# A message ring, one-hots shared with ScalarE and attribute sums moved one pass earlier in a graph network's two gather passes

## The reference

```python
# second layer: sum over the edges that end in a node, and their count
h = features * (deg_out ** (-0.5))[:, None] @ weight
rst = segment_sum(h[src], dst) * (deg_in ** (-0.5))[:, None] + bias
# third layer: a message of each edge
msg = relu(x[src] + edge_attr)
agg = segment_sum(msg, dst)
h = relu((x + agg) @ W1 + b1) @ W2 + b2
# fourth layer, input norm: needs edge_attr summed by node, and edge_attr.T @ edge_attr
h = concatenate([x[col], edge_attr], axis=1)
h = relu(_bn(h @ W1a, g1a, b1a))
```

## Time and profile before

| | us |
|---|---|
| median of three executions | 9768.53 |
| profiled execution, its own time | 9783.38 |
| its span, first to last instruction | 9781.0 |
| second pass, first gather to last `add_block` | 2960.3 to 5054.7 |
| third pass, first gather to last `add_block` | 5109.5 to 7282.1 |

### The profile page before, as it was taken

One profiled execution on the slowest core, in us unless ns is written; L12 is line 12 of the kernel. 1 busy time (PEld: TensorE's weight loads), 2 busy tenths in 40 slices (PEclk: granted clock), 3 DMA queues, 4 the chain that ended last, 5 costly groups with the idle time before them and its releaser, 6 DMA issues. The chain is left out here.

```text
span 9781.0 us, 179091 instructions
## 1 busy us (share of the span) xinstructions
PE 6958.7 (71%) x25668; PEld 5296.4 (54%) x25669; DVE 5640.9 (58%) x22552; ACT 2074.7 (21%) x8123; POOL 6775.9 (69%) x7038
## 2 busy tenths in 40 slices
PE   2676667675768888888845555555567888888886
PEld 1555555554546666666633333333345666666664
DVE  8777777776984444444455555555554444444444
ACT  4344444443120000000002222222221222221222
POOL 0677777776737777777757777777745777777773
PEclk8555555555655555555555555555565555555556
DMA  6333333333642222222212222222212333333334
GB/s 109 96 105 105 106 105 109 103 108 94 138 93 64 55 55 55 55 55 53 57 40 54 55 53 53 53 53 53 54 23 74 80 80 82 80 82 80 82 80 34
DMA packets 625950, 724.44 MB, mean 74 GB/s; under 512 B 403289, under 2 KB 431609, under 8 KB 624766
## 3 DMA queue, kind: packets, MB, share of 16 engines
q1 hardware_dynamic: 394414, 429.07, 16.5%
q0 software_dynamic: 216064, 278.76, 12.9%
q10 hardware_dynamic: 14544, 8.74, 0.5%
HBM read 576.22 MB, written 139.85 MB: 73 GB/s over the span
## 5 line engine op out<-in xcount | busy, mean ns | idle before, releaser
L1293 POOL DMA_INDIRECT arena<-node_table,idx x3328 | 3165.0, 951 | 1091.6 <-issue 788.5
L1231 PE MATMUL banks<-arena,onehot 128*128 x7040 | 2497.3, 472 | 1245.2 <-DVE onehot L1171 608.5
L1231 PEld LDWEIGHTS banks<-arena,onehot 128*128 128x128 f32 x7040 | 1758.4, 311 | 1879.6 <-issue 1673.7
L1414 POOL DMA_INDIRECT arena<-node_table,arena x1760 | 1665.3, 946 | 552.0 <-issue 378.8
L978 POOL DMA_INDIRECT sorted_edges<-arena,idx x1664 | 1616.4, 971 | 615.7 <-issue 575.2
L1171 DVE TENSOR_SCALAR onehot<-iota_row,block_base,edge_tables 128x128 f32<-128x128 f32 x3520 | 1251.8, 357 | 608.5 <-ACTq L1277 464.1
L923 PE MATMUL banks<-arena,onehot 128*128 x3520 | 1103.9, 424 | 563.2 <-DVE onehot L872 550.3
L923 PEld LDWEIGHTS banks<-arena,onehot 128*128 128x128 f32 x3520 | 883.6, 314 | 783.2 <-issue 776.5
L1179 DVE TENSOR_TENSOR arena<-arena,banks 128x65 f32 (+1 forms) x3520 | 895.5, 254 | 583.4 <-PE banks L1231 543.7
L1390 PE MATMUL banks<-arena 128*128 128x64 f32 x3520 | 1214.1, 448 | 0.0
L1385 PE MATMUL banks<-arena 128*64 128x65 f32 x3520 | 843.0, 343 | 396.2 <-ACT arena L1401 387.5
(11 more groups left out here) (291 smaller groups left out, 6021.2 us busy)
## 6 DMA issues: line engine op xcount, KB each, us to landing
arena<-sorted_edges SPq DMA_DIRECT2D x220, 524.0 KB
arena<-in_attr_t SPq DMA_DIRECT2D x208, 512.0 KB
arena<-sorted_edges SPq DMA_DIRECT2D x110, 528.0 KB, 4.3
arena<-row_keys SPq DMA_DIRECT2D x110, 512.0 KB
arena<-in_attr_pairs SPq DMA_DIRECT2D x104, 512.0 KB
arena<-node_table,idx POOLq DMA_INDIRECT x3328, 2.4
arena<-node_table,arena POOLq DMA_INDIRECT x1760, 2.4
sorted_edges<-arena,idx POOLq DMA_INDIRECT x1664
```

Of the source, the lines that this page charges most:

```text
L1231: nc.tensor.matmul(to, m.onehot[:, j % 4, :], rows, start=True, stop=True).then_inc(s["summed"], 1)
L1293: nc.gpsimd.indirect_dma_start(slot(j), None, m.table, bass.IndirectOffsetOnAxis(ap=m.idx[:, j:j + 1], axis=0)).then_inc(gathered[j % 32], 16)
L1414: nc.gpsimd.indirect_dma_start(slots[:, j % SLOTS, 0:D], None, m.table, bass.IndirectOffsetOnAxis(ap=rec_i[:, j % SLOTS, REC_DST:REC], axis=0)
```

## The change

- The sums of the edge attributes by node move from the third pass to the second. The second pass's ring slot is now 129 floats wide (`WIDE`): gathered row, attribute row, a one. SyncE loads the attributes straight into the ring, in pieces of 64 floats. Its products have 129 columns, and a block's sums stand 130 floats apart (`STEP`).
- The Gram matrix moves from the second pass to the third: TensorE multiplies the attribute tile j with itself before step j, for j below 1664, and at every sixteenth waits for the attributes of its chunk.
- In the third pass, messages are made by step and not by tile: VectorE adds gathered row and attributes of the step's own tile into a ring of eight (`messages`), ScalarE applies the relu there, TensorE multiplies 64 columns. So there are 1760 messages where there were 1664.
- VectorE waits for landed tiles at each eighth step in the third pass too. SyncE does the counting, tile by tile, between its own loads. VectorE loads 25 numbers of the plan at each eighth step (eight blocks, eight tiles, eight slots, one last tile) where it loaded 16.
- ScalarE makes the one-hot of each odd step as relu(1 - |lane + offset|): four small activations for the offsets at every eighth step, after loading 16 numbers of the plan, and two activations of 128 x 128 for each odd step.
- GpSimd waits on `landed` at each eighth gather in both passes.

```diff
-            if layer == 1:
-                v.memset(m.pair[:, :, 0:RW], 0.0).then_inc(s["blank"], 1)
-            def add_attr(i, j):
-                c = j // CH
-                dve.wait_ge(gathered[j % 32], i * (RING // 32 * 16) + j // 32 * 16 + 16)
-                if j % CH == 0:
-                    dve.wait_ge(attr_in[c], i * 16 + 16)
-                v.tensor_tensor(slot(j), slot(j), m.third_ring[:, 1, j * D:(j + 1) * D], ALU.add).then_inc(s["sum"], 1)
+            def add_attr(base, j, slots):
+                k = base + j
+                dve.wait_ge(s["summed"], ahead(k - 8, SLACK))
+                v.tensor_tensor(m.messages[:, j % 8, :], rows[:, bass.ds(slots[j] * D, D)], attrs[:, bass.ds(slots[j] * D, D)],
+                                ALU.add).then_inc(s["sum"], 1)
...
+                            last = bounded_values(nc, ENG.DVE, plan[32:33, bass.ds(base + j + 7, 1)], TP - 1)[0]
                             blocks += group(nc, ENG.DVE, plan, 0, base + j, SPARE - 1)
                             tiles += group(nc, ENG.DVE, plan, 1, base + j, TP - 1)
+                            if layer == 2:
+                                slots += group(nc, ENG.DVE, plan, 2, base + j, RING - 1)
+                            dve.wait_ge(s["landed"], last + 1 + EARLY)
+                        if layer == 2:
+                            add_attr(base, j, slots)
+                        if layer == 1 or j % 2 == 0:
+                            match(base, j, tiles, blocks)
...
+        def count(engine, i, j):
+            i, j = i + j // RING, j % RING
+            if j % CH == 0:
+                engine.wait_ge(attr_in[j // CH], i * 16 + 16)
+            engine.wait_ge(gathered[j % 32], i * (RING // 32 * 16) + j // 32 * 16 + 16)
+            engine.sem_inc(s["landed"], 1)
...
+                def rounds(i, last):
+                    for c in range(CHUNKS):
+                        if c + 1 < CHUNKS:
+                            load(sp, i, c + 1)
+                        elif not last:
+                            load(sp, i + 1, 0)
+                        for j in range(c * CH + 8, min(c * CH + CH + 8, RING) if last else c * CH + CH + 8):
+                            count(sp, i, j)
...
+            def add_gram(i, j):
+                if j % CH == 0:
+                    pe.wait_ge(attr_in[j // CH], i * 16 + 16)
+                attr = attrs[:, j * D:(j + 1) * D]
+                nc.tensor.matmul(m.psum[GRAM][0:D, 0:D], attr, attr, start=False, stop=False, skip_group_check=True)
+            with pe.Fori(0, ROUNDS) as i:
+                for j in range(RING):
+                    if layer == 2:
+                        add_gram(i, j)
+                    step(i * RING, j, numbers)
...
+                def aim(base, j):
+                    blocks = group(nc, ENG.Activation, plan, 0, base + j, SPARE - 1)
+                    tiles = group(nc, ENG.Activation, plan, 1, base + j, TP - 1)
+                    act.wait_ge(s["odd"], base + j + EARLY)
+                    for q in range(1, 8, 2):
+                        a_.activation(m.place[:, q:q + 1], targets[:, bass.ds(tiles[q], 1)], ACT.Identity, scale=-1.0,
+                                      bias=m.block_base[:, bass.ds(blocks[q], 1)]).then_inc(s["aimed"], 2)
+                    act.wait_ge(s["aimed"], base + j + 8)
+                def steps(base, units):
+                    for j in range(0, units, 2):
+                        if j % 8 == 0:
+                            aim(base, j)
+                        odd = j + 1
+                        apart = m.junk[:, odd // 2 % 2, :]
+                        a_.activation(apart, m.iota_row[:, :], ACT.Abs, bias=m.place[:, odd % 8:odd % 8 + 1]).then_inc(s["apart"], 2)
+                        relu(base + j, j)
+                        act.wait_ge(s["apart"], base + j + 2)
+                        act.wait_ge(s["summed"], base + odd - 3 + SLACK)
+                        settle(act)
+                        a_.activation(m.onehot[:, odd % 4, :], apart, ACT.Relu, scale=-1.0, bias=m.ones[:, 0:1]).then_inc(s["odd"], 2)
+                        relu(base + odd, odd)
```

More of the change, by code:

```diff
@@ new lines, in _ @@
+            if layer == 1:
+                with sp.Fori(0, ROUNDS) as i:
+                    for c in range(CHUNKS):
+                        load(sp, i, c)
+            else:
+                def rounds(i, last):
+                    for c in range(CHUNKS):
+                        if c + 1 < CHUNKS:
[4 more added lines that the diff above has]
+                            count(sp, i, j)
+                sp.sem_inc(s["landed"], EARLY)
+                load(sp, 0, 0)
+                for j in range(8):
+                    count(sp, 0, j)
+                with sp.Fori(0, ROUNDS - 1) as i:
+                    rounds(i, False)
+                rounds(ROUNDS - 1, True)
@@ L1250, in _ @@
-            with pe.Fori(0, ROUNDS) as i:
-                beats(i)
+                if layer == 1:
+                    if j % 8 == 0:
+                        numbers += group(nc, ENG.PE, plan, 2, k, RING - 1)
+                    frm = m.second_ring[:, bass.ds(numbers[j] * WIDE, WIDE)]
+                else:
+                    pe.wait_ge(s["message"], k + 1)
+                    frm = m.messages[:, j % 8, :]
+                if layer == 1:
+                    pe.wait_ge(s["onehot"], ahead(k, EARLY))
+                else:
+                    pe.wait_ge(s["odd" if j % 2 else "onehot"], ahead(k, EARLY))
@@ L1263, in _ @@
             a_ = nc.scalar
-            act.sem_inc(s["message"], EARLY)
-            if layer == 2:
-                a_.activation(m.pair[:, :, D:2 * D], m.zero[:, 0:D].unsqueeze(1).to_broadcast([P, NB, D]),
+            if layer == 1:
+                a_.activation(m.pair[:, :, D:WIDE], m.zero[:, 0:RW].unsqueeze(1).to_broadcast([P, NB, RW]),
                               ACT.Copy).then_inc(s["blank"], 1)
-                with act.Fori(0, ROUNDS) as i:
-                    for j in range(RING):
-                        act.wait_ge(s["sum"], i * RING + j + 1 + 2 * CH)
-                        a_.activation(slot(j), slot(j), ACT.Relu).then_inc(s["message"], 1)
-            else:
                 act.sem_inc(s["landed"], EARLY)
@@ L1275, in _, with relu @@
                     for j in range(RING):
-                        act.wait_ge(gathered[j % 32], i * (RING // 32 * 16) + j // 32 * 16 + 16)
-                        act.sem_inc(s["landed"], 1)
+                        count(act, i, j)
+            else:
+                def relu(k, j):
+                    act.wait_ge(s["sum"], k + 1)
+                    row = m.messages[:, j % 8, :]
+                    a_.activation(row, row, ACT.Relu).then_inc(s["message"], 1)
+                act.sem_inc(s["odd"], EARLY)
+                def aim(base, j):
[8 more added lines that the diff above has]
+                    for j in range(0, units, 2):
+                        if j % 8 == 0:
+                            aim(base, j)
[8 more added lines that the diff above has]
+                        relu(base + odd, odd)
+                with act.Fori(0, ROUNDS) as i:
+                    steps(i * RING, RING)
+                with act.Fori(0, LAG // TAIL) as i:
+                    steps(i * TAIL + TP, TAIL)
                 act.wait_ge(s["gram_done"], 1)
```

123 lines of the change are left out of this document (49 added, 74 removed).

## The result

The changed kernel takes 9976.77 us (median of four executions, 9973.42 to 9978.43) against 9767.57 us (9766.39 to 9771.14, four executions of the kernel before in the same session). The ratio is 1.0211, 95% interval 1.0199 to 1.0224. The prediction said 9767 with a range of 9735 to 9812; the time lies 165 us above that range. It is nearest to the rival that had been given 1 in 10: the steps and no longer the gathers set the pace of the third pass.

What follows compares the result with a forecast made beforehand. Gathers, one per about 1.25 us, were taken to pace both passes, leaving only the third pass's 79.5 us end uncovered. Terms 0.6 - 5 + 3 = -1.4 us gave 9782.0 profiled, median 9767; range 9735 to 9812.

Steps and rivals of the forecast that it cites:

- the rival that had been given 1 in 10: Third pass: tight handovers make eight steps exceed 10.07 us, so steps set the pace; about 9890 us, chance 0.10.
- VectorE's price for the plan's numbers: Third pass, each eighth step: loading 25 plan numbers idles VectorE 2.1 us, where 16 cost 1.33.
- waits some 0.4 us for the first message: Third pass, TensorE: 8.24 us for eight steps plus this wait, about 8.65, covered by 10.07 us of gathers.
- the round ends: Third pass: only three loop ends behind the last gather were priced, 0.7 us each.
- ScalarE: Third pass: offsets, loads, odd one-hots and relus take 7.1 us for eight steps, bounds 5.9 to 9.2.
- The end: Third pass behind the last gather: attribute waits limit the lead; 3 us more, bounds 11 less to 28 more.
- G - 5.6: Third pass, G being the last gather: the last 96 steps begin 5.6 us before it.
- The forecast of G + 82.6: Third pass: last sum 82.6 us behind the last gather G, where it was 79.5 before.
- The 7.1: Third pass's end: ScalarE's 7.1 us for eight steps sets the pace of the last 96, 85 us.
- The rival that had the steps run up to 97 ahead: Third pass ends like the second, 10.2 us behind its last gather; 69 us less, about 9698, chance 0.05.
- The second pass: Lost Gram product and wider sums stay hidden under the gathers, attribute pieces cost nothing; its end adds 0.6 us.
- The gathers: Third pass: fewer VectorE one-hots save 5 us over 1664 gathers, bounds 0 to 22; message adds keep their price.

Runs made afterwards that it cites:

- the fifth load: Changed kernel plus one more used VectorE load of eight block numbers at each eighth step of the third pass: 10125.28 us.
- spread loads: Changed kernel with VectorE's three third-pass loads of eight at steps 2, 4 and 6, fetching the next group's numbers: 9792.34 us, ratio 1.0026.
- the lagging Gram product: Changed kernel with loads spread in both passes and the third pass's Gram product of tile j - 96 at step j: 9760.09 us, ratio 0.9995.

## Why the prediction was wrong, by its own steps

**The step that failed** is VectorE's price for the plan's numbers: "16 of them cost an idle 1.33 us at each eighth step; 25 then cost 2.1". It priced numbers; what costs is the load instruction, 0.53 to 0.82 us each for one number or for eight, and two became four. 3.54 us were measured, not 2.1; the fifth load's 0.62 us confirms the price, and the moved load's 182 us what hangs on it. The same section of the earlier trace rows that gave the 1.33 could have been split: the queue's rows of before show it as two loads of 596 ns. The Trainium skill (DMA: Bandwidth & Descriptors, Latency and other measured facts) gives a floor of about 600 ns for one such load. For eight numbers the trace agrees with its 608 ns; the load of one number, at 534 ns, and ScalarE's, at 547, lie below that floor. Weighing that line ahead of the run would have raised the same doubt.

**The step that followed from it** is TensorE's: "waits some 0.4 us for the first message", 8.65 for eight steps. TensorE had work in hand for 2.3 us after VectorE began to load (6261.0 to 6263.3), and waited 2.2. The rival gave it three steps in hand; it was two. That rival, the third, had named the point from which it decides, TensorE's waits at 1.8 us a group rather than 0.4; they came to 2.2. It had looked for the cause on ScalarE, and gave 10.5 us for eight steps: measured were 10.46. That this came so close is luck, for its 10.5 was not worked out from the loads. Its time, 9890, was 87 us short of the measured one.

**A term at nothing: the round ends.** The prediction priced loop ends only behind the last gather, three at 0.7 us. The 12 round ends ahead of it were covered as long as the gathers set the pace; when the steps did, they cost 5.1 us each, 61 of the 148 us. The other 87 are close to the 89 that the rival had for groups of 10.5 us.

**ScalarE.** The aims took 0.85 us (1.0 predicted), Abs 0.40 and the one-hot's relu 0.39 (0.38). These held. Its two loads took 0.55 us each. ScalarE is not the bound in the changed kernel, neither up to the last gather nor behind it; its relus are what TensorE waits for once the loads are spread. Abs, relu and identity follow each other, and the last table load of the trace (ACT_TABLE_LOAD, 1.28 us) stands at 2899.85, ahead of both passes. By the Trainium skill (ScalarE: Activation LUTs, Table sets: the hidden batching unit) these three are in every set, so none was to be expected, and the trace agrees.

**The end.** That the Gram product's wait for attributes limits the lead is shown by TensorE's 85.2 us of such waits with spread loads, and its last Gram product came 6.8 us before the last gather, where the forecast had the steps reach their last 96 at G - 5.6. In the changed kernel itself that wait is absent, 3.7 us in all by the profile's page, since the steps are behind anyway:

```profile
L1261 PE MATMUL banks<-arena 128*64 128x64 f32 x3328 | 793.2, 342 | 3.7 <-DMA arena<-in_attr_t 3.7
```

The forecast of G + 82.6 missed by 43 us in two terms. The 96 last steps begin at G + 20.95 instead of G - 5.6, for the steps are late throughout (26.5 us). And they take 104.6 us instead of 88.2, as TensorE's timeline shows with eight products and a wait in each group:

```profile
7379.69 5.17 PE L1254 MATMUL banks<-edge_tables,onehot 128*128 128x64 f32 x16 [3.75 <-DVE arena L1194]
7388.27 3.40 PE L1254 MATMUL banks<-edge_tables,onehot 128*128 128x64 f32 x10 [3.42 <-DVE arena L1194]
```

That is 8.6 us and not 7.1 (16.4 us in all). The 7.1 were ScalarE's; the bound here too is VectorE, whose gap at the head of each of these groups is again 3.54 us. The rival that had the steps run up to 97 ahead was right about what lies behind that wait: without Gram products the end is 11.1 us and the time 9696.76 us.

**The second pass** came out as predicted in its main point: its end stays at 5054.5, a sum of 129 columns takes 0.29 us, and the attribute loads in pieces of 256 bytes land in 4.5 us (4.3 was taken) and delay nobody. One term was missing: its gathers became longer, 951 ns against 946 in the kernel before profiled again (948 in the first execution), and first to last they take 2087.7 us where that took 2079.8.

**The gathers.** Five us less were predicted for the third pass; with the kernel before profiled again it is 2087.9 against 2079.1 us, 9 less. The second pass lost 8, so the kernel gained nothing by it. The prediction took the message adds to keep their price, and the one-hots to give back 3.5 ns. The first part is not borne out: the adds are still in the third pass, where the surplus has gone, and there are none in the second, where it now stands. In all these traces the longer gathers are in the pass whose products and sums have 128 or 129 columns, by 1 to 6 ns; these moved from the third pass to the second. Other things moved with them, and no run changes the width alone, so that cause is argued and not shown. The second part has some support. Two pairs of kernels differ in who makes the odd one-hots (and with it in ScalarE's loads and offsets): with all of them on VectorE a gather of the third pass took 949 ns in both, with half of them 946 and 945. But in those two executions the gathers of the fourth pass, which nothing touches, were longer too (945 against 944 ns), and so were those of the first (970 against 968); 1 to 2 ns remain for the one-hots. Where the steps set the pace, no difference shows (946 ns either way).

**What stays open** beside this is why the gap at a loop end is 6.6 us and not 3.5, and TensorE's wait there 7.6 and not 2.2; and what orders VectorE's and TensorE's turns so that eight steps take 9.6 us with all one-hots on VectorE and the loads spread.

## What to carry to other kernels

Count the load instructions for registers, not the numbers they load, and put them where their engine waits anyway: one of them moved by four steps was worth 182 us here. A stretch that is paced by something else covers added work only up to a point, and beyond it each tenth of a microsecond is paid in full, so ask of several small additions what they make together; each of the two here, loads and Gram product, was free alone up to the last gather. And where the steps are more than the items they wait for, the limit for an end without a tail is lower than the one for an unbroken pace (9.5 against 10.07 us here); kernels between the two had their last sum 65 to 106 us behind the last gather. Count the loop ends into that pace: they hide under a faster pacemaker and come out, 4 to 8 us each here, when the steps set the pace.

## What the runs showed of the hardware

- In the changed kernel a load of one plan number into a register takes 534 ns on VectorE, of eight 608 ns in the median and up to 828 (547 on ScalarE), and the instructions behind it wait; a single number with its bounds check pays two register operations of up to 190 ns on top.
- A round end of a loop of 128 unrolled steps lengthened the group of eight across it from 10.5 to 15.6 us in the changed kernel, and from 9.3 to 16.5 with spread loads and the lagging Gram product.
- The same kernel's gathers averaged 954 ns in one profiled execution and 951 in another, and the two differed by 19 us in all. In the slower one the gathers of the fourth pass were longer as well (946 against 944 ns), so such an offset can be seen in a pass that no change touches. A row of a few ns read from one execution isn't a property of the kernel.
